# A twelve-layer perceiver kernel: new DMA order in the last expert layer, 128-wide tiles in the first, and two changes of instruction order in the attention layers

## The reference, cut to what matters

```python
# L2x, L3x: cross attention of 128 queries over 12544 context rows, 16 heads of 16
K = ctx @ Wk;  V = ctx @ Wv
w = softmax(q @ K.T / 4 + mask);  x = x + (w @ V) @ Wo

# L0a: gated linear attention; L2a: elu-feature linear attention (both causal)
A = (q_h @ k_h.T) * causal;  num = A @ [v_h, 1];  o = num[:, :16] / num[:, 16]

# L1a: layer norm of q and k in each head of 16, then causal softmax attention
q = ln(q) * w + b;  k = ln(k) * w + b
p = softmax(q_h @ k_h.T / 4, causal);  o = p @ v_h

# L1f: weights dequantised from integers, x + mlp(x)
W = (q - 128) * scale

# L0f: 8 experts of 704 inner columns, gated by silu; L2f: 8 of 1024
h = silu(x @ W1[e].T) * (x @ W2[e].T);  y += weight[e] * (h @ W3[e].T)

# L3f: 8 gated experts of 1024 inner columns, each for at most 20 + 20 dispatched tokens
```

## Time and profile before

| | us |
|---|---|
| three runs: lowest, median, highest | 1709.24, 1710.79, 1713.70 |
| the profiled execution's own time | 1712.22 |
| its span in the trace | 1710.4 |
| PE busy in the span | 1572.2 (92%) |
| DVE, ACT, POOL busy | 1084.5, 855.1, 15.1 |
| mean granted clock of TensorE, share of full speed | 0.981 |

### The profile page before, as it was taken

One profiled execution on the slowest core, in us unless ns is written; L12 is line 12 of the kernel. 1 busy time (PEld: TensorE's weight loads), 2 busy tenths in 40 slices (PEclk: granted clock), 3 DMA queues, 4 the chain that ended last, 5 costly groups with the idle time before them and its releaser, 6 DMA issues.

```text
span 1710.4 us, 34666 instructions
## 1 busy us (share of the span) xinstructions
PE 1572.2 (92%) x14196; PEld 1167.7 (68%) x14196; DVE 1084.5 (63%) x2038; ACT 855.1 (50%) x1249; POOL 15.1 (1%) x23
## 2 busy tenths in 40 slices
PE   6998978998999999999987898899999999998897
PEld 5776467775667777677766666667777777776664
DVE  5422322546787878878787423777888787878631
ACT  3021032104777676767676121577666666667610
POOL 0000000100000000000000000000000000000000
PEclk9999999999999999999999899999999999999999
DMA  9666845236243335334230365434343242424344
GB/s 384 213 195 203 287 129 172 120 129 243 88 164 109 145 142 181 134 129 164 88 130 8 123 230 214 167 109 161 137 157 143 97 152 88 152 88 160 143 177 202
DMA packets 39308, 267.65 MB, mean 156 GB/s; under 512 B 4760, under 2 KB 5016, under 8 KB 30360
## 3 DMA queue, kind: packets, MB, share of 16 engines
q1 hardware_dynamic: 39160, 265.55, 43.1%
HBM read 159.49 MB, written 3.28 MB: 95 GB/s over the span
## 4 chain that ended last, share of the span: by engine, by line
PE 74%; DVE 10%; DMA 8%; issue 5%; ACT 3%; SPq 1%; POOL 1%; DVEq 0%; ACTq 0%
PE T L790 12%; PE O L812 11%; PE S L776 7%; PE T L748 7%; PE O L790 6%; PE T L761 5%; PE S L648 4%; PE O L748 3%; PE O L947 3%; PE S L1096 3%; PE T L643 2%; DVE sc L1605 2%; DMA ctx_in<-in_ctx_cols 2%; PE O L761 2%; DVE pT L1571 2%
## 5 line engine op out<-in xcount | busy, mean ns | idle before, releaser
L1605 DVE CUSTOM_DVE_ANT_0 sc<-S,mask_bias,small 128x896 f32<-128x896 f32 x336 | 380.0, 1144 | 12.2 <-PE S L776 9.5
L1209 ACT ACTIVATE sc<-sc,small 128x1792 f32<-128x1792 f32 x168 | 299.8, 1786 | 12.4 <-DVE small L1605 9.5
L1195 ACT ACTIVATE pT<-T 128x512 f32<-128x512 f32 x293 | 169.1, 595 | 149.2 <-PE T L790 148.8
L812 PE MATMUL O<-pT,arena 128*32 128x128 f32 x6272 | 198.7, 278 | 44.6 <-DVE pT L1571 44.6
L790 PE MATMUL T<-consts,sc 128*128 128x128 f32 x1552 | 231.7, 280 | 1.7 <-ACT sc L1209 0.8
L812 PEld LDWEIGHTS O<-pT,arena 128*32 128x32 f32 x6272 | 168.5, 111 | 84.6 <-issue 51.8
L790 PEld LDWEIGHTS T<-consts,sc 128*128 128x128 f32 x1552 | 170.7, 141 | 64.2 <-issue 31.2
L1571 DVE COPY pT<-T 128x512 f32<-128x512 f32 x225 | 151.3, 687 | 94.4 <-PE T L790 94.3
L776 PE MATMUL S<-keys,q 64*128 64x512 f32 (+1 forms) x896 | 151.1, 415 | 14.9 <-DVE small L1605 13.7
L1195 ACT ACTIVATE pT<-O 128x512 f32<-128x512 f32 x155 | 92.2, 595 | 88.6 <-PE O L790 88.1
L1605 DVE CUSTOM_DVE_ANT_0 packs<-S,mask_bias,small 128x896 f32<-128x896 f32 x112 | 128.3, 1145 | 0.0
(11 more groups left out here) (348 smaller groups left out, 1980.9 us busy)
## 6 DMA issues: line engine op xcount, KB each, us to landing
keys<-keys_hl SPq DMA_DIRECT2D x112, 896.0 KB, 7.9
ctx_in<-in_ctx_cols SPq DMA_DIRECT2D x46, 896.0 KB, 8.1
wide<-in_ctx_rows SPq DMA_DIRECT2D x14, 896.0 KB, 5.7
wide<-in_up_L0f SPq DMA_DIRECT2D x8, 1408.0 KB, 9.5
sc<-in_ctx_cols SPq DMA_DIRECT2D x10, 896.0 KB, 11.0
wide<-in_up_L2f SPq DMA_DIRECT2D x8, 1024.0 KB, 6.6
wide<-in_down_L2f SPq DMA_DIRECT2D x8, 1024.0 KB, 4.8
wide<-in_up_L3f SPq DMA_DIRECT2D x4, 2048.0 KB, 8.9
```

The lines of the kernel that those rows point to most:

```text
L812: last = mm(O2[32 * g:32 * g + 32, 1, at:at + P], vv[:, c % 2, b, j * 32:(j + 1) * 32], pT2[:, t * P:(t + 1) * P], start=(b < 4), stop=(b ...
L1195: nc.scalar.activation(pT2[:, g * BANK:(g + 1) * BANK], ring(plan, u), ACT.Copy).then_inc(s["t_act"], 1)
L1209: nc.scalar.activation(weights_of(n), weights_of(n), ACT.Exp, bias=n_best[c % 2][:, h:h + 1], scale=-1.0, accum_out=l_new[c % 2][:, h:h + ...
L1605: V.tensor_tensor_reduce(weights_of(n)[:, i * HC:(i + 1) * HC], S4f[:, n % 2 * 2 * BANK:n % 2 * 2 * BANK + HC], mask_bias[:, i * HC:(i + 1 ...
```

## The change

It has four parts. (1) SP in L3f issues the up weights of pairs 2 and 3 ahead of the down weights of both. (2) `tiles` cuts the inner columns of L0f in 5 tiles of 128 and one of 64 in place of 8 of 88; the down weights are laid out anew, padded to 6 tiles of 128 rows. L2f's tiles stay 8 of 128. (3) In the cross layers T6 is copied by ACT, T2 goes ahead of the first half of the scores, T5 ahead of the second, and the quad behind T6. (4) L0a, L2a and L1a work bank by bank; L1a takes its root on ACT, with one Newton step on DVE, drops two copies, and gives three early units to L1f; blocks of `warm` are cut.

```diff
+def tiles(layer):
+    return [(f // P, min(P, FF[layer] - f)) for f in range(0, FF[layer], P)]
...
 def emptied_by(u):
-    return "act" if u[0] == "T" and u[2] not in (0, 1, TURNS - 1) else "dve"
+    return "act" if u[0] == "T" and u[2] not in (0, 1) else "dve"
...
             def load_down(layer, e, b):
-                F = FF[layer]
-                m = KD * (2 if layer in GATED else 1) * F
-                sp.dma_start(fb[0:F // E, b, m:m + E * D], a[f"down_{layer}"][bass.ds(e, 1)].rearrange(
+                m = KD * (2 if layer in GATED else 1) * FF[layer]
+                sp.dma_start(fb[:, b, m:m + len(tiles(layer)) * D], a[f"down_{layer}"][bass.ds(e, 1)].rearrange(
...
                 elif layer == "L3f":
-                    for e in range(4, E):
-                        sp.wait_ge(s["g_ready"], 2 * (e // 2 - 1))
-                        sp.dma_start(expert_up(e % 4), a["up_L3f"][e]).then_inc(s[f"up_in{e % 4}"], 16)
-                        if e % 2:
-                            sp.wait_ge(s["y_ready"], e // 2 - 1)
-                            for d in (e - 1, e):
-                                sp.dma_start(expert_down(d % 4), a["down_L3f"][d]).then_inc(s[f"down_in{d % 4}"], 16)
+                    def load_ups(p):
+                        sp.wait_ge(s["g_ready"], 2 * (p - 1))
+                        for e in (2 * p, 2 * p + 1):
+                            sp.dma_start(expert_up(e % 4), a["up_L3f"][e]).then_inc(s[f"up_in{e % 4}"], 16)
+                    def load_downs(p):
+                        sp.wait_ge(s["y_ready"], p - 1)
+                        for e in (2 * p, 2 * p + 1):
+                            sp.dma_start(expert_down(e % 4), a["down_L3f"][e]).then_inc(s[f"down_in{e % 4}"], 16)
+                    load_ups(2)
+                    load_ups(3)
+                    load_downs(2)
+                    load_downs(3)
...
-                    pe.wait_ge(s["t_dve"], plan.emptied(("T", m, TURNS - 1)))
-                    pe.wait_ge(s["t_act"], plan.emptied(("T", m, TURNS - 2)))
+                    pe.wait_ge(s["t_dve"], plan.emptied(("T", m, 1)))
+                    pe.wait_ge(s["t_act"], plan.emptied(("T", m, TURNS - 1)))
...
-                warm(S4[:, 0], 20)
+                warm(S4[:, 0], 14)
                 need(pe, "dve", f"{layer}.onehot")
...
-                    for t in range(E):
-                        last = mm(O2[:, b, 0:D], hidT[0:F // E, t, :], w[:, t, :], start=(t == 0), stop=(t == E - 1))
+                    for t, rows in tiles(layer):
+                        last = mm(O2[:, b, 0:D], hidT[0:rows, t, :], w[0:rows, t, :], start=(t == 0),
+                                  stop=(t == tiles(layer)[-1][0]))
...
                 elif layer in ("L1a", "L2a"):
-                    qkv(layer, xT, 16 if layer == "L1a" else 2)
+                    qkv(layer, xT, 2)
...
                         early("L3x", 3, O2[:, 1], 2)
+                        early("L3x", 4, T2[:, 1], 3)
...
-                    done("pe", heads_products(halfT, blk), f"{layer}.A_ps")
+                    heads_products(layer, "A")
...
-                        warm(O2[:, 1], 9)
-                    need(pe, "dve", f"{layer}.AT")
-                    for h in range(H):
+                    for b in range(4):
+                        need(pe, "dve", f"{layer}.AT{b}")
+                        for h in range(4 * b, 4 * b + 4):
...
-                    done("pe", heads_products(halfT, blk), f"{layer}.S_ps")
-                    early("L2x", 5, T2[:, 1])
-                    early("L2x", 6, O2[:, 0])
-                    warm(O2[:, 1], 24)
-                    need(pe, "act", f"{layer}.p")
+                    heads_products(layer, "S")
+                    warm(T2[:, 1], 4)
                     for b in range(4):
-                        last = transposes(S4[:, b], mats[:, b * BANK:(b + 1) * BANK], 4)
+                        need(pe, "act", f"{layer}.p{b}")
+                        done("pe", transposes(S4[:, b], mats[:, b * BANK:(b + 1) * BANK], 4), f"{layer}.turned{b}")
+                        if b:
+                            need(pe, "act", f"{layer}.pT{b - 1}")
+                            for h in range(4 * b - 4, 4 * b):
...
-                    warm(T2[:, 0], 34)
+                    for b, bank in ((4, T2[:, 0]), (5, T2[:, 1]), (6, O2[:, 1])):
+                        early("L2x", b, bank)
+                    warm(S4[:, 3], 8)
                     need(pe, "dve", f"{layer}.w")
...
+                    need(act, "dve", f"{layer}.var2")
+                    done("act", nc.scalar.activation(head_b, head_a, ACT.Sqrt), f"{layer}.std2")
+                    take_early("L2x", 3, T2[:, 1])
...
+                    V.tensor_copy(vaug[:, :, 0:DH], S4[:, 1, 0:D].rearrange("p (h d) -> p h d", h=H))
+                    need(dve, "act", f"{layer}.std2")
+                    link(V.reciprocal(head_b, head_b))
+                    link(V.tensor_tensor(vsum, head_b, head_b, ALU.mult))
+                    link(V.tensor_tensor(vsum, vsum, head_a, ALU.mult))
+                    link(V.tensor_scalar(vsum, vsum, -0.5, 1.5, ALU.mult, ALU.add))
+                    link(V.tensor_tensor(head_b, head_b, vsum, ALU.mult))
...
+                    for b in range(4):
+                        four, of = mats3[:, 4 * b:4 * b + 4], head_a[:, 4 * b:4 * b + 4]
+                        need(dve, "pe", f"{layer}.S{b}")
...
```

163 lines of the change are left out of this document (88 added, 75 removed).

## The result

The changed kernel takes 1669.74 us (median of four runs, 1667.09 to 1671.98), against 1712.24 (1709.24 to 1713.92, four runs) before: a ratio of 0.9753, 95% interval 0.973 to 0.9777. The forecast was 1669.6. The profiled execution took 1671.98, its span is 1670.0. So the sum was right to 1 us. It was not right term by term: errors of up to 5 us cancelled, which was luck, and this is the lesson of the case.

What follows compares the result with a forecast made beforehand. PE, busy in 92% of the span, was taken to bound the kernel. Terms summed to -41.2 us, taking the profiled 1712.2 to 1671.0 and the median 1710.8 to 1669.6; range 1656 to 1683.

Steps and rivals of the forecast that it cites:

- L3f, loads: In L3f, up weights 6 and 7 issued earlier: last up product starts 5.4 us sooner and runs 2.7 shorter, -8.1 us.
- L0f (-10.8): In L0f, six down products for eight, fewer turned tiles, no wait for up weights: steps of 8.0 us, -10.8 us.
- the rival that the loads get no faster: Rival in L0f: weight loads still take 9.8 us, so the term is -5.0 and the time 1675; 12%.
- L1a (-8.9): In L1a, root on ACT and bank-by-bank work end the chain 9.9 us earlier, less 1.0 for the clock: -8.9 us.
- I give back 1.0 for the clock: In L1a, 1.0 us taken off the 9.9 us gain in case TensorE's clock falls.
- The rival of the clock: Rival in L1a: TensorE falls to 1.2 GHz as PE stands in gaps, giving back 4 to 5 us: 1674; 20%.
- L2a and L0a (-4.2): DVE's masking by banks no longer holds the head products: -2.4 us in L0a, -1.8 in L2a behind an early unit.
- Cross layers (-7.5): In L2x and L3x, T6's earlier copy on ACT shortens waiting pairs: -6.2 us in L2x's full chunks, -1.3 elsewhere.
- ACT as the bound (3%): Rival in the cross layers: PE waits for ACT's copies, 0.60 us in each of 112 pairs, slower at 1744 us; 3%.
- nothing gained (13%): Rival: the cross layers give nothing, since another wait takes the place of this one, 1677 us; 13%.
- twice the gain (10%): Rival: the cross layers give twice the forecast gain, 1662 us; 10%.
- L1f (-0.7): In L1f, fewer warm matmuls plus three early units end at 363.3, so DVE's weights at 364.2 decide: -0.7 us.

Runs made afterwards that it cites:

- the two warm kernels: Changed kernel with warm matmuls added in L1a's gaps: 30 before the turn, 6 between banks (1671.26 us); or 17, then 4, 2 and 2 (1671.7 us).

## Why the prediction was right, and where it was not

**L3f, loads (-8.1).** Right: the stage gives 8.0, 5.3 of start (38.8 to 33.5) and 2.7 of clock (9.73 to 7.02), the two numbers of the step. The 14 warm matmuls for 20: -0.9 in this pair of runs for -1.0, but L3a scatters by 3 us over the runs, so it is not shown. I had called the 0.23 us of one its time at the low clock; the granted clock is 1.00 there (1639 to 1644), and 0.23 is the time at the full one. The term does not change by it.

**L0f (-10.8).** Measured -8.1, inside the bounds of -5.0 and -11.5. The DMA wait went, as the step said, and the rival that the loads get no faster is out. The step that failed is "a matmul of 256 columns costs by its columns; 128 rows for 88 I cost at nothing". This holds for 128 and 88, but the sixth tile has 64. Where the number of rows changes, the weight load stands twice for 0.33, and six down matmuls take 2.88 us, not 2.6. With the tile filled up a step is 7.98 us in place of 8.33; seven steps and the last down product make the missing 2.7 us. Of the filled kernel's gain PE's new waits for up weights take a part back.

**L1a (-8.9).** Measured -7.8. The walk over ACT was right: from the q, k, v product to the end of the root 10.2 us (forecast 10.2), to q and k ready 13.7 (13.5). What failed is the size of "I give back 1.0 for the clock". PE had stood 3.5 us when q and k came, so it turned them at 1.2 GHz (1.11 us for 0.66), and the 22 warm matmuls behind ran late into the scores: from the turn to the scores 4.3 us for 3.4. From the scores to the output step it was 14.5 for the 13.2 forecast, since the last two groups of head products took 1.73 and 1.87 us where a full clock takes about 1.0. That makes some 2.1 us against the 1.0 of the term, and the run with 17 warm matmuls gave back 2.9. By the nine profiles with this code (34.2 to 35.4 us) -7.8 is the best case and the part is worth 6.5 to 7.8. The rival of the clock (20%) so came true in good part; it had priced 4 to 5. The Trainium skill (TensorE: Matmul & The Clock Gate, Why this matters for your kernels) advises against gaps between bursts of matmuls; the two warm kernels agree with it, and show that the filling has to fit. The table load took 1.28 us and ACT went on at once, so the 2.66 with a drain that the Trainium skill (ScalarE: Activation LUTs, What ACT_TABLE_LOAD costs) gives was not seen.

**L2a and L0a (-4.2).** Measured -6.7 and -3.8. For L0a the piece from the scores to L0f is 16.9 us for 19.6, -2.7; the rest of the -3.8 lies ahead of the change. In L2a the step "an early unit stands ahead of the scores and holds them 0.5: -1.8" was blind to the clock. From L2x's last multiply to the head products it is 26.1 us for 28.3, so the wait gave 2.2, near the term; from the head products to L2f it is 11.3 for 15.7, and these 4.5 us are the slow stretch. I named TensorE's clock as a risk of the change and did not look where the kernel before already lost by it. Its windows would have shown 0.50 in 967 to 975.

**Cross layers (-7.5).** L2x gave 7.0, with four chunks 1.26 shorter and one 0.98 where I had 1.3 for each, and the walk through a pair was right to 0.04 us. (Five chunks at 1.3 make 6.5, not the 6.2 of my sum.) L3x was to give some tenths: its full chunks give none, but for 0.4 in the sixth. "About 0.2 for ACT in the waiting pairs" was low: the multiply still waits 28.9 us in 48 places, 0.6 each. ACT as the bound (3%), nothing gained (13%) and twice the gain (10%) are out.

**L1f (-0.7).** Measured -1.8, though the changed code took 16.4 to 17.3 in the other runs, -1.0 to -1.8. The stage scatters by nearly 1 us, and the rest of the difference is not explained.

**The sum.** Measured less forecast, in us: L3a and L3f +0.2, L0f +2.7, L1a +1.1, L1f -1.1, start and L0a -1.4, L2a -4.9, cross layers +3.2, stages that the change does not touch +0.8: +0.6, and -40.5 for -41.2 with rounding. So the time came out to 1 us by luck, because errors of up to 5 us cancelled. Of them, L0f and L1a have causes that the runs show; L2a's is a slow stretch whose cause is open; the start, L1x and L3x are scatter.

**The signs.** Three of my signs did not come as written. L0f's steps are 8.33 and not 8.0. L1a takes 13.5 us from DVE's first work on the scores to its output step and not 12, with a granted clock of 0.84 from the q, k, v product to the tail, which I had named a sign of being wrong. And L3x's pairs take 8.9 to 10.4 us; I had read 9.6 to 10.3 before, where they took 9.0 to 10.3, and their sum in a chunk is the same.

## What to carry to other kernels

When you cost an added or shortened matmul, look at its row count beside its neighbours': a tile of another height costs its own gap at either side, and padding with zeros may be cheaper. Look for stretches of low clock in the kernel before, behind every wait that a change removes: in L2a before, some 10 us at 1.2 GHz followed a stand of 0.75 us. Compare with more than one profile before you call the stand the cause. Walk a steady pair or step row by row, for that forecast held to 0.04 us here, and trust stage totals only to the scatter of what lies between.
